# Attention with experts behind it: row maxima one slot and a third ahead of the scores, a new written-out order, and rotations on GpSimd alone before the first batch

## The reference

```
q, k, v = split(x @ W_qkv)                 # 16 heads of 16 channels
q, k = rope(q), rope(k)
w = softmax(mask(q @ k.T / sqrt(16)))      # causal
x = layernorm(x + (w @ v) @ W_o)
gate = softmax(x @ Wg + bg); keep the two largest of 8, divide by their sum
out = layernorm(x + sum_e gate_e * (x @ We[e].T + be[e]))
```

## Time and profile before

| what | value |
|---|---|
| median of 3 runs | 3246.15 us (3246.06 to 3248.67) |
| profiled execution | 3247.9 us, span 3246.2 us, mean granted clock of TensorE 0.979 |
| TensorE matmul busy | 3110.3 us (96%) |
| VectorE busy | 2684.6 us (83%) |
| ScalarE busy | 1885.3 us (58%) |
| GpSimd busy | 1198.2 us (37%) |

### The profile page before, as it was taken

How to read it: one execution, slowest core, us unless ns; L and a number is a source line. 1 busy time by engine, 2 the same in 40 slices (tenths; PEclk the granted TensorE clock), 3 DMA queues, 4 the chain that set the end, 5 groups by cost and what they waited for, 6 DMA issues and landing times.

```text
span 3246.2 us, 58552 instructions
## 1 busy us (share of the span) xinstructions
PE 3110.3 (96%) x18752; PEld 1712.3 (53%) x18752; DVE 2684.6 (83%) x8456; ACT 1885.3 (58%) x4257; POOL 1198.2 (37%) x1410
## 2 busy tenths in 40 slices
PE   4789999999999999999999999999999999999987
PEld 2234555555555555555555555555555555555555
DVE  6877888888888888888988888888888888888745
...
DMA packets 174819, 210.95 MB, mean 65 GB/s; under 512 B 26008, under 2 KB 124592, under 8 KB 174256
## 3 DMA queue, kind: packets, MB, share of 16 engines
...
## 4 chain that ended last, share of the span: by engine, by line
PE 84%; DVE 8%; issue 3%; ACT 2%; POOL 1%; DMA 1%; ACTq 0%; SPq 0%; DVEq 0%; POOLq 0%
PE bank L917 22%; PE attend L1012 15%; PE scores L990 14%; PE bank L974 14%; PE bank L954 6%; PE bank L1036 3%; PE bank L963 3%; DVE bank L775 2%; PE bank L1020 1%; PE bank L942 1%; DVE maxima L778 1%; PE bank L1027 1%; PE bank L1044 1%; ACT weights L651 1%; PE bank L1068 1%
## 5 line engine op out<-in xcount | busy, mean ns | idle before, releaser
L651 ACT ACTIVATE weights<-scores 128x512 f32<-128x512 f32 (+3 forms) x3072 | 1333.5, 495 | 886.0 <-PE scores L990 872.7
L775 DVE CUSTOM_DVE_ANT_0 bank<-bank,far_q 128x128 f32<-128x128 f32 (+3 forms) x2048 | 963.1, 512 | 202.7 <-PE bank L974 187.2
L974 PE MATMUL bank<-k_stack,q_stack 96*128 96x512 bf16 (+3 forms) x3072 | 803.6, 333 | 31.7 <-DVE maxima L775 10.5
L990 PE MATMUL scores<-q_stack,k_stack 99*128 99x512 bf16 (+3 forms) x3072 | 821.1, 328 | 10.6 <-ACT weights L651 6.9
L571 POOL TENSOR_SCALAR_AFFINE_SELECT weights<-weights 128x512 f32<-128x512 f32 x512 | 325.4, 637 | 1269.4 <-ACT weights L651 1269.1
L778 DVE TENSOR_REDUCE maxima<-bank 128x1 f32<-128x512 f32 x1024 | 643.9, 682 | 71.2 <-PE bank L974 70.9
L1012 PE MATMUL attend<-weights,values 128*32 128x512 f32 (+3 forms) x6144 | 579.2, 492 | 1.0 <-POOL weights L571 0.9
L990 PEld LDWEIGHTS scores<-q_stack,k_stack 99*128 99x128 bf16 x3072 | 280.1, 97 | 411.8 <-ACT weights L651 154.6
L974 PEld LDWEIGHTS bank<-k_stack,q_stack 96*128 96x128 bf16 x3072 | 276.9, 98 | 400.6 <-issue 153.6
L917 PE MATMUL bank<-wexp_hi,zT_hi 128*128 128x512 f32 x1024 | 381.7, 454 | 11.1 <-DVE lowrows L795 11.1
L891 DVE SCALAR_TENSOR_TENSOR z<-bank,picked,z 128x256 f32<-128x256 f32 x512 | 247.5, 483 | 113.8 <-PE bank L917 104.9
...
## 6 DMA issues: line engine op xcount, KB each, us to landing
parts_scratch<-parts SPq DMA_DIRECT2D x128, 384.0 KB, 2.5
q_stack<-parts_scratch SPq DMA_DIRECT2D x384, 128.0 KB, 7.1
k_stack<-parts_scratch SPq DMA_DIRECT2D x384, 128.0 KB, 7.7
...
```

The costliest lines, as they stand in the source:

```text
L651: act.activation(weights[:, n % NW, hh, c0:CH], st[(QUAD * n + hh) % NS][:, c0:CH], ACT.Exp, scale=DH ** -0.5).then_inc(S["weights_ready"], 1)
L775: dve.tensor_tensor_reduce(out=b[:, 0:w], in0=b[:, 0:w], in1=far_q[:, CH - w:CH], scale=1.0, scalar=-SENTINEL, op0=ALU.add, op1=ALU.max, a ...
L974: pe.matmul(b[:, 0:w], q_stack[0:ROWS, n, hh, qt * P:(qt + 1) * P], k_stack[0:ROWS, n, hh, kc * CH:kc * CH + w], start=True, stop=True).th ...
L990: pe.matmul(st[(QUAD * n + hh) % NS][:, c0:CH], k_stack[0:MROWS, s, hh, kb * P:(kb + 1) * P], q_stack[0:MROWS, s, hh, qc * CH + c0:(qc + 1 ...
```

## The change

Of slot 3 of the turn's maxima (those of slot 1 of the attention), the items from LATE_B = 4 on, and MC.3 and MT.3, move to the beginning of the turn that uses them. So maxima lead their scores by one slot and a third. B.0 to B.2 follow each a slot later than before, and MT.2, for slot 0 of the next batch, stands in the last line of ORDER. "pre" takes the maxima of slot 0 and of four items of slot 1 only; "last" receives the other eight items. ORDER is written anew throughout, with the same steps. In "pre", TURN is gone: GpSimd does both products and the sum, and VectorE both subtractions. The expert weights are loaded at the end of "pre" (ScalarE's queue), and WSPLIT stands in line ST.5 of stage "first". No step is computed differently.

Core of the diff (of ORDER the lines at its beginning, around the gates and at its end):

```diff
@@ -40,6 +40,7 @@
 NS = 3
 NW = 3
 DMA = 16
+LATE_B = 4
 BITEM = [(qt, kc) for kc in range(T // CH) for qt in range(CH // P * kc, TILES)]
@@ ORDER @@
-XL.0 XL.1 XT.0 XL.2 XT.1 XL.3 B.0.0.0 B.0.0.1 MC.3
-ST.0.0 ST.0.1 B.0.0.2 B.0.0.3 B.0.1.0 B.0.1.1 ST.0.2 ST.0.3 MASK.0 B.0.1.2 PV.46 PV.47 YE.3.1 B.0.1.3
-ST.1.0 B.0.2.0 ST.1.1 B.0.2.1 ST.1.2 B.0.2.2 ST.1.3 MASK.1
...
-ST.10.0 ST.10.1 GL.0 ST.10.2 N1A.1 ST.10.3 B.0.11.0 MASK.10 B.0.11.1 B.0.11.2 B.0.11.3 PV.8 PV.9 B.1.0.0 YT.0.0
-ST.11.0 ST.11.1 GLT.0 ST.11.2 ST.11.3 MASK.11 B.1.0.1 B.1.0.2
-ST.12.0 MC.0 B.1.0.3 B.1.1.0 ST.12.1 ST.12.2 ST.12.3 MASK.12 CAST.0.2.0 PV.10 PV.11 YE.0.1 GA.0
-ST.13.0 B.1.1.1 GB.0 ST.13.1 ST.13.2 QK.0.3 B.1.1.2 ST.13.3 MASK.13
...
-ST.45.0 ST.45.1 B.3.8.2 B.3.8.3 ST.45.2 VP.0 B.3.9.0 YT.3.0 B.3.9.1 ST.45.3 MASK.45
-ST.46.0 N2A.1 ST.46.1 B.3.9.2 VP.1 B.3.9.3 B.3.10.0 B.3.10.1 ST.46.2 ST.46.3 MASK.46 PV.44 PV.45
-ST.47.0 B.3.10.2 B.3.10.3 B.3.11.0 VP.2 B.3.11.1 ST.47.1 B.3.11.2 VP.3 ST.47.2 ST.47.3 MASK.47 B.3.11.3
+XL.0 XL.1 XT.0 XL.2 XT.1 B.3.4.0
+ST.0.0 XL.3 B.3.4.1 XR.0 ST.0.1 ST.0.2 B.3.4.2 B.3.4.3 ST.0.3 MASK.0 B.3.5.0 PV.46 XR.1 PV.47 YE.3.1 B.3.5.1
+ST.1.0 ST.1.1 ST.1.2 B.3.5.2 B.3.5.3 ST.1.3 YT.3.1 MASK.1
...
+ST.5.0 ST.5.1 ST.5.2 ROPE.0.0 CAST.0.0.0 B.3.9.2 B.3.9.3 B.3.10.0 WO.0.0 WO.0.1 R1.0 HT.1.0 B.3.10.1 ST.5.3
+  WSPLIT
+ST.6.0 QK.0.1 B.3.10.2 B.3.10.3 ST.6.1 CAST.0.0.1 ST.6.2 ST.6.3 HT.1.1 ROPE.0.1 B.3.11.0 B.3.11.1 B.3.11.2 PV.4
+  PV.5
...
+ST.10.0 ZT.0.0 ZT.0.1 ST.10.1 ST.10.2 ST.10.3 MASK.10 MT.3 QK.0.2 B.0.2.3 B.0.3.0 CAST.0.1.1 ROPE.0.2 PV.8
+  B.0.3.1 GL.0 B.0.3.2 B.0.3.3 PV.9
+ST.11.0 ST.11.1 ST.11.2 B.0.4.0 B.0.4.1 ST.11.3 MASK.11
+ST.12.0 N1A.1 GLT.0 B.0.4.2 GA.0 ST.12.1 GB.0 ST.12.2 ST.12.3 B.0.4.3 CAST.0.2.0 QK.0.3 B.0.5.0 MASK.12 PV.10
+  PV.11 GT.0 YE.0.1
+ST.13.0 B.0.5.1 CAST.0.2.1 B.0.5.2 ST.13.1 ST.13.2 BE.0.0 BE.0.1 ROPE.0.3 MOE.0.0.0 ST.13.3 B.0.5.3 MOE.0.0.1
+  B.0.6.0 MOE.0.0.2 B.0.6.1 MOE.0.0.3 MOE.0.1.0 B.0.6.2 B.0.6.3 MASK.13
...
+ST.20.0 B.1.1.2 B.1.1.3 B.1.2.0 ST.20.1 ST.20.2 B.1.2.1 B.1.2.2 ST.20.3 MT.0 MASK.20 PV.18 PV.19
+ST.21.0 ST.21.1 B.1.2.3 B.1.3.0 B.1.3.1 ST.21.2 ST.21.3 MASK.21 MOE.0.2.2 ROPE.1.0 MOE.0.2.3
...
+ST.44.0 MC.2 MOE.1.3.3 ST.44.1 ST.44.2 ST.44.3 MASK.44 N2.1 PV.42 PV.43
+ST.45.0 B.3.0.2 ST.45.1 ST.45.2 B.3.0.3 B.3.1.0 R2.1 YT.3.0 ST.45.3 MASK.45 B.3.1.1 B.3.1.2
+ST.46.0 ST.46.1 ST.46.2 B.3.1.3 ST.46.3 MASK.46 B.3.2.0 PV.44 PV.45 N2A.1 B.3.2.1 B.3.2.2
+ST.47.0 MT.2 VP.2 B.3.2.3 B.3.3.0 B.3.3.1 ST.47.1 ST.47.2 ST.47.3 MASK.47 VP.3 B.3.3.2 B.3.3.3
@@ -155,10 +160,12 @@
     kind, s = step[0], step[1] if len(step) > 1 else 0
     ahead, behind = seg in ("first", "mid"), seg in ("mid", "last", "post")
     attend = seg in ("first", "mid", "last")
+    if kind == "WSPLIT":
+        return seg == "first"
     if step in (("PV", SLOTS * ITEMS - 2), ("PV", SLOTS * ITEMS - 1), ("YE", SLOTS - 1, 1), ("YT", SLOTS - 1, 1)):
         return behind
-    if step in (("MC", SLOTS - 1), ("MT", SLOTS - 1)):
-        return seg in ("mid", "last")
+    if step in (("MC", SLOTS - 1), ("MT", SLOTS - 1)) or (kind == "B" and s == SLOTS - 1 and step[2] >= LATE_B):
+        return attend
     if kind in ("B", "MC", "MT"):
         return ahead or (seg == "last" and s < 2)
     if kind == "LOAD":
@@ -182,20 +189,15 @@
             if m < len(halves):
                 out += [("QK", *halves[m]), ("ROPE", *halves[m])]
             if m:
-                out += [("CAST", *halves[m - 1], 0)]
-            if m < len(halves):
-                out += [("TURN", *halves[m])]
-            if m:
-                out += [("CAST", *halves[m - 1], 1)]
+                out += [("CAST", *halves[m - 1], n) for n in range(2)]
             if m == 4:
                 out += [("LOAD", 0)]
             if m >= 5:
                 out += [("VP", m - 5)]
             if m == 6:
                 out += [("LOAD", 1)]
-        out += [("LOAD", 2), ("WSPLIT",)] + scores + [("MC", 0), ("MT", 0)]
-        out += [("B", 1, it, hh) for it in range(ITEMS) for hh in range(QUAD)]
-        out += [("MC", 1), ("MT", 1)]
+        out += [("LOAD", 2)] + scores + [("MC", 0), ("MT", 0)]
+        out += [("B", 1, it, hh) for it in range(LATE_B) for hh in range(QUAD)]
         return out
     return [step for step in ORDER if belongs(step, seg)]
 
@@ -266,8 +268,6 @@
                 add(f"parts_stored{step[2] % 2}", seg, step)
             if step[0] == "ROPE":
                 add("turning", seg, step)
-                if seg == "pre":
-                    add("sines", seg, step)
     return book
 
 
@@ -404,7 +404,7 @@
         pv = ctx.enter_context(nc.psum_tensor("attend", [P, CH], F32))
         bk = [ctx.enter_context(nc.psum_tensor(f"bank{i}", [P, CH], F32)) for i in range(NB)]
 
-        names = [*COUNTED, "link", "rest_ready", "parts_ready", "turning", "sines", "sp_waits", "pool_waits", "dve_waits",
+        names = [*COUNTED, "link", "rest_ready", "parts_ready", "turning", "sp_waits", "pool_waits", "dve_waits",
                  "zeroed", "zeroed_v", "bias_zeroed", "bias_split", "const_v", "const_p", "ident_ready", "w_loaded", "we_loaded", "hi_split", "w_split"]
         names += [f"{n}{i}" for n in ("stack", "maxrow") for i in range(SLOTS)]
         names += [f"{n}{i}" for n in ("x_loaded", "resid_loaded", "stored", "parts_stored") for i in range(2)]
@@ -554,14 +554,11 @@
                     s, k = a
                     x1, ch = rope[:, k % 2], k // 2
                     pool.wait_ge(S["swapped"], c.at("swapped", step))
-                    turned = pool.tensor_tensor(x1, x1, cos[:, ch * CH:(ch + 1) * CH], ALU.mult)
-                    if c.seg == "pre":
-                        turned.then_inc(S["turning"], 1)
-                    else:
-                        pool.tensor_tensor(rope_swap[:, :], rope_swap[:, :], sin[:, ch * CH:(ch + 1) * CH], ALU.mult) \
-                            .then_inc(S["turning"], 1)
-                        pool.wait_ge(S["turning"], c.at("turning", step))
-                        pool.tensor_tensor(x1, x1, rope_swap[:, :], ALU.add).then_inc(S["rotated"], 1)
+                    pool.tensor_tensor(x1, x1, cos[:, ch * CH:(ch + 1) * CH], ALU.mult)
+                    pool.tensor_tensor(rope_swap[:, :], rope_swap[:, :], sin[:, ch * CH:(ch + 1) * CH], ALU.mult) \
+                        .then_inc(S["turning"], 1)
+                    pool.wait_ge(S["turning"], c.at("turning", step))
+                    pool.tensor_tensor(x1, x1, rope_swap[:, :], ALU.add).then_inc(S["rotated"], 1)
                 elif kind == "MASK":
                     (n,) = a
                     kb, qc = ITEM[n % ITEMS]
@@ -570,7 +567,7 @@
                     block = weights[:, n % NW, :, c0:c0 + P]
                     pool.affine_select(out=block, in_=block, compare_op=ALU.is_ge, fill=no_weight, base=0,
                                        pattern=[[0, QUAD], [1, P]], channel_multiplier=-1).then_inc(S["masked"], 1)
-                elif kind == "CAST" and (c.seg != "pre" or a[2]):
+                elif kind == "CAST" and c.seg != "pre":
                     rest(pool, c, *a)
                 elif kind in ("R1", "R2"):
                     (g,) = a
@@ -602,7 +599,10 @@
                 step = (kind, *a)
                 b = bk[bank(c.seg, step)] if kind in BANKED else None
                 fr = free[bank(c.seg, step)] if kind in BANKED else None
-                if kind == "XT":
+                if kind == "END" and c.seg == "pre":
+                    for kt in range(KT):
+                        act.dma_start(staged[kt], w_exp[kt * P:(kt + 1) * P, :]).then_inc(S["we_loaded"], DMA)
+                elif kind == "XT":
                     (j,) = a
                     filled(act, c, step)
                     act.activation(xT[:, :, 2 * P * j:2 * P * (j + 1)], b[:, :].rearrange("p (k n) -> p k n", k=KT),
@@ -702,8 +702,6 @@
             act.wait_ge(S["bias_zeroed"], 1)
             act.dma_start(bgate[0:NE, :], b_gate.rearrange("(n o) -> n o", o=1)).then_inc(S["w_loaded"], DMA)
             act.wait_ge(S["w_loaded"], W_LOADS * DMA)
-            for kt in range(KT):
-                act.dma_start(staged[kt], w_exp[kt * P:(kt + 1) * P, :]).then_inc(S["we_loaded"], DMA)
             run(act, work)
 
         @block.vector
@@ -778,7 +776,7 @@
                         dve.tensor_reduce(dst, b[:, 0:w], AX.X, ALU.max).then_inc(fr, 1)
                 elif kind == "MC":
                     (s,) = a
-                    emptied(dve, c, ("B", s, ITEMS - 1, QUAD - 1), prev=s == SLOTS - 1 and c.seg != "pre")
+                    emptied(dve, c, ("B", s, ITEMS - 1, QUAD - 1))
                     m = maxima[:, s % 2].rearrange("p (h t) -> p h t", h=QUAD)[:, :, 4:TILES]
                     dve.tensor_tensor(m, m, maxima_hi[:, s % 2].rearrange("p (h t) -> p h t", h=QUAD), ALU.max) \
                         .then_inc(S["maxima_ready"], 1)
@@ -800,17 +798,7 @@
                         dve.wait_ge(S["rotated"], c.below("rotated", step, 1))
```

(12 more changed lines are left out.)

90 lines of the change are left out of this document (42 added, 48 removed).

## The result

The kernel after takes 3269.09 us (median of 4 runs, 3266.96 to 3270.39); the kernel before took 3246.11 on the same chip. The ratio is 1.0064, with a 95% interval of 1.005 to 1.0078: slower, as forecast, and by 23 us where 7 were forecast. The profiled execution took 3270.39 us, its span is 3268.7.

A forecast was written before the change was run, and what follows sets the result against it. TensorE was taken to bound the steady batch, VectorE's maxima and a chain of short steps the start. Start -29, first batch +9, last +4 and +1, steady batches +22 gave +7 us: 3253.5 us, own range 3244 to 3264, all 3228 to 3272.

The forecast's parts named there:

- (a): Start: the expert weights' split leaves it, VectorE doing the last rotated half's cast and second subtraction instead; gain 6.8 us.
- (d): Start, rotations: with three operations on GpSimd a half takes 6.2 us where it took 5.91; +1.5 us.
- (b): Start: the 32 maxima of slot 1 from item 4 on, and their merging, leave it; gain 16.9 us.
- (c): Start: the chain from the last maximum to x's first transposition goes, x being there when wanted; gain 6.7 us.
- the clock's term: First batch: one microsecond for TensorE's lower clock, part of the +9 us there.
- Rival 2: First batch: the weights' split stops it for 14 us or more, TensorE's clock falling after; 3259 us, chance 0.10.
- (e): Turn of the loop: x's load queued behind MT.2 makes TensorE wait 2.3 us instead of 0.51; +1.8 us a batch.
- (f): Steady batch: TensorE's 0.74 us wait at the expert matmul behind the maxima's transpose goes; -0.7 us a batch.
- (g): Steady batch, gates: B.0.4.2 between GLT.0 and GA.0 on VectorE lengthens the chain to 4.8 us; +0.5 us a batch.
- (h): Steady batch: the rest of the order, with denser maxima around the experts; 0 us, from -1 to +1.
- Rival 1: Turn of the loop costs TensorE little, last steps overlapping x's load, freer VectorE saving later waits; 3232 us, chance 0.30.
- Rivals 3 and 4: 3: start's rotations at 6.9 us a half, 3259 us, chance 0.10; 4: rows late for slots 0, 1, 3, 3287 us, 0.05.

The follow-up runs named there:

- e11: Kernel before, with the expert weights' two loads issued behind the third half's second cast instead of ahead of everything; 3245.57 us, ratio 0.9981.
- e4: Kernel after, with the expert weights' split and loads put back between the rotations and the first maxima; 3272.11 us, ratio 1.0066.
- e6: Kernel after, with the rotations shared between GpSimd and VectorE again as in the kernel before; 3266.52 us, ratio 1.0048.
- e5: Kernel after, with x's first two loads of the next batch issued on SyncE just ahead of its wait at MT.2; 3231.39 us, ratio 0.994.
- e7: Kernel after, with the weights' split cut into eight pieces spread over lines ST.2 to ST.41 of the first batch; 3268.69 us, ratio 1.0057.
- e3: Kernel after, with MT.2 moved by two maxima, ahead of B.3.2.1 and B.3.2.2; 3236.99 us, ratio 0.996.
- e9: Kernel after, with x's loads ahead of SyncE's wait at MT.2, the weights' split in eight pieces and VP.3 as last step; 3226.41 us, ratio 0.9927.
- e1: Kernel after, with MT.2 moved from the start of line ST.47 to line ST.44, behind MOE.1.3.3; 3244.97 us, ratio 0.9984.

## Why the prediction came out as it did

**The start: -35.8 us, forecast -29.** Its pieces: the first maximum comes 13.6 us earlier (81.77 to 68.21), where (a) and (d) gave 5.3. 4.8 of these are the loads of the weights, which the prediction moved without asking what they had held up; e11 shows it. 8.2 lie between the last shuffle and the first maximum (17.95 to 9.73), for (a)'s 6.8. The rest, 0.5, is (d), whose sign was wrong: a half takes 5.60 us where 6.2 were taken and 5.91 were before (the first half alone got longer, 4.90 for 3.57). In the kernel after VectorE's subtractions lie at the edges of GpSimd's products, and GpSimd runs on:

```profile
31.10 0.67 DVE L459 TENSOR_TENSOR rope<-rope,parts 128x512 f32<-128x512 f32 x1
31.29 1.61 POOL L557 TENSOR_TENSOR rope<-rope,cos_sb 128x512 f32<-128x512 f32 x1 [0.97 <-DVE rope_swap L800]
32.47 0.98 DVE L461 TENSOR_TENSOR parts<-rope,parts 128x512 bf16<-128x512 f32 x1 [0.70 <-ACT parts L625]
32.86 1.71 POOL L558 TENSOR_TENSOR rope_swap<-rope_swap,sin_sb 128x512 f32<-128x512 f32 x1
34.65 1.26 POOL L561 TENSOR_TENSOR rope<-rope,rope_swap 128x512 f32<-128x512 f32 x1
```

Against 1.27 undisturbed GpSimd loses 0.34 and 0.44 us, not the whole 0.67 and 0.98 of the two subtractions. The first subtraction began 0.19 us before the first product, which ran beside it for 0.48 us and lost 0.34; the second began while that product was still running, and lasted 0.98 us for some 0.7. This is compatible with the exclusion that the Trainium skill's page SBUF — State Buffer (Who interferes with whom) states, by which the one that comes first goes first; the 6.3 us a half worked out with it, every subtraction wholly between two of GpSimd's, did not come. Then (b): from the first maximum to the end of the last one are 33.2 us for 50, -16.7 against -16.9. And (c): XT.0 starts 1.2 us behind the last maximum in place of 6.7, a gain of 5.5 for 6.7; x was not there when it was wanted, though (c) said so: its loads were issued at 96.19, behind slot 0's rows, and TensorE waits 3.1 us.

**The first batch: +15.5, forecast +9.** The wait behind the split was taken as 6 and is 5.95 us. The size of the clock's term was wrong: 1 us was taken, and 20.4 us of half clock are there (from 127.6, 161.8 and 202.7). The first and longest of these stretches begins a microsecond ahead of the long wait, behind one of 1.6 us for ScalarE's exponentials at 127.05. Rival 2's mechanism in part, though with half of its 14 us of wait. With the block out of the way 5.1 us over the 153.6 remain (e4). 1.5 of them are the wait for x that ends this batch (2.0 us for 0.5), which the prediction counted for the steady batches alone; the other 3.6 no experiment divides.

**The steady batch: +2.5, forecast +1.6.** The terms of waiting came near: from MT.2 to XT.0 7.15 us for 7.1, and in (e) a wait of 2.0 us for a forecast 2.3, so +1.5 for +1.8; (f) -0.7, as put; (g) +0.25 for +0.5. (h) 0. That would be +1.05 a batch. The missing term is the clock at each meeting, 1.7 us in 13 of them: 22 us in all. The step that failed is (e), which priced the wait at its own length and called the rest TensorE's unchanged work; rival 2 had the clock at the split, but nowhere was it asked what a wait of 2 us in every batch does to it. In the 14 steady batches together the waits of (f) were 10.4 us and are gone, those of (g) are 3.6: 13 x (1.5 + 1.7) - 10.4 + 3.6 = 34.8 us, for 34.7 measured.

**The last batch: +8.3, forecast +5.** TensorE is busy for 9.1 us more (165.98 against 156.88). One part is again a wait with half clock behind it, the gates' transposition; in e6 the same wait has nothing behind it. First the kernel after (the stretch, then the transposition in the timeline), then e6 likewise:

```profile
3039.20:3049.40 10.20, 9.77 (x27) 6.05 (x27) 5.71 (x10) 2.83 (x6) 0.96 (x2) 0.50 0.00 0
```

```profile
3039.63 1.03 PE L1056 MATMUL bank<-ident,gates_parts 128*24 128x128 f32 x4 [2.42 <-DVE gates_parts L865]
```

```profile
3040.70:3050.90 10.20, 9.75 (x46) 6.91 (x47) 9.53 (x18) 2.83 (x6) 0.99 (x2) 1.00 0.00 0
```

```profile
3041.15 0.61 PE L1075 MATMUL bank<-ident,gates_parts 128*24 128x128 f32 x4 [2.43 <-DVE gates_parts L884]
```

27 matmuls in 10.2 us against 46, and a last batch of 172.8 against 168.6 us: 4.2 us for one such stretch. Without it the last batch is 4.1 us longer than before, against the forecast 5.

**The sum.** -6.8 (start), +6.5 (first), +12.7 (steady), +3.1 (last with what follows) against the forecast make the 15.5 us between +7 and +22.5. The measured 3269.09 us is above the forecast's own range of 3244 to 3264 and inside the range of all, 3228 to 3272. So the direction came with the mechanism of (e), but the distance had luck in it: 22 us of misses one way, above all the lower clock, which the sum had as a single microsecond, were met by 7 us the other way, of which 4.8 are the weights' loads. Two figures of the forecast do not follow from its own terms: a batch of +2.2 gives 3262 and not 3264, and rival 2's 14 us of wait in place of 6 give 3261.5 and not 3259. **The rivals.** Rival 1 was wrong for this kernel: the load was not hidden by the last steps. With x in time (e5) the new order is 0.5 us a batch shorter at its bare length than the old one (190.8 against 191.3 in the steady batch that ends without that wait), which is what (f) and (g) give, -0.7 + 0.25; rival 1's other half, later waits saved by a freer VectorE, isn't needed for it and isn't shown. The shorter lead of the maxima costs nothing in the waits, as the prediction said. Rivals 3 and 4 did not come; no wait for the rows stands in the table.

What stays open: why a wait of 2.4 us in the last batch is followed by 10.2 us (the kernel after, e4, e7), 6.8 (e3, e5, e9), 3.4 (e1) or no half clock at all (e6) in kernels that have the same steps there, why the first meeting of the new order never had a fall, and what of the work around a wait matters beside its length.
